# A graph kernel on Trainium2: in the first edge layer GpSimd also waits for the sums of two groups earlier before it gathers a group

## The reference

```python
edge_index = jnp.stack([src, dst])
h = jnp.maximum(_layernorm(x), 0.0)
# layer 0, a graph convolution
xw = h @ W
dinv = rsqrt(segment_sum(ones, dst) + ...)        # 1/sqrt(degree)
x = x + relu(segment_sum(xw[src] * (dinv[src] * dinv[dst])[:, None], dst) + b)
h = jnp.maximum(_layernorm(x), 0.0)
# layer 1, attention over the edges, 8 heads of 16
q, k, v = h[src] @ Wq.T + bq, h[dst] @ Wk.T + bk, h[dst] @ Wv.T + bv
e = exp(clip(einsum('ehd,ehd->eh', q, k) / sqrt(16), -10, 10))
out = segment_sum(e / (segment_sum(e, src)[src] + 1e-8) * v, src)
x = x + layernorm(out + h) * gamma + beta
```

## Time and profile before

| | us |
|---|---|
| timed runs, median of 3 | 2273.32 |
| timed runs, lowest and highest | 2272.0, 2273.41 |
| recorded execution, its span (the page gives no other time for it) | 2940.6 |

### The profile page before, as it was taken

How to read it: one execution, slowest core, us unless ns; L and a number is a source line. 1 busy time by engine, 2 the same in 40 slices (tenths; PEclk the granted TensorE clock), 3 DMA queues, 4 the chain that set the end, 5 groups by cost and what they waited for, 6 DMA issues and landing times. The chain is left out here.

```text
span 2940.6 us, 44304 instructions
## 1 busy us (share of the span) xinstructions
PE 1840.2 (63%) x10257; PEld 1461.4 (50%) x10258; DVE 1874.7 (64%) x5089; ACT 1279.6 (44%) x3362; POOL 1551.0 (53%) x1594
## 2 busy tenths in 40 slices
PE   5323346767576676677776767676666676666662
PEld 4323334544344444344454656566556665656662
DVE  9858775655455755455775666666666666666666
ACT  8524345755465565556653323333223332322333
POOL 0256655665556565565434555545455555555544
PEclk7756667877778787878887888888888888888886
DMA  3211111111111111111116444445444544444453
GB/s 105 62 41 42 43 39 39 45 42 38 38 38 45 38 41 41 39 44 39 33 68 185 126 125 127 127 122 131 119 121 124 132 123 122 125 123 123 126 122 55
DMA packets 234145, 244.06 MB, mean 83 GB/s; under 512 B 32925, under 2 KB 195229, under 8 KB 233989
## 3 DMA queue, kind: packets, MB, share of 16 engines
q0 software_dynamic: 61136, 147.00, 18.5%
q1 hardware_dynamic: 142357, 81.55, 10.8%
q10 hardware_dynamic: 30624, 15.21, 2.2%
HBM read 225.01 MB, written 18.62 MB: 83 GB/s over the span
## 5 line engine op out<-in xcount | busy, mean ns | idle before, releaser
L303 POOL DMA_INDIRECT rows<-y_tab,idx x832 | 795.6, 956 | 589.8 <-issue 307.9
L1340 POOL DMA_INDIRECT x<-kv_tab,kv_idx x672 | 682.7, 1016 | 623.0 <-DVE msg L1392 403.9
L1563 PE MATMUL ps_kv<-kv_s,hot_low 128*128 x1362 | 406.0, 443 | 168.9 <-DVE hot_low L1364 90.0
L780 ACT ACTIVATE sort_v<-sort_t,staged,minus 128x128 f16<-128x128 f16 x914 | 360.7, 480 | 309.1 <-remote 243.1
L872 PE MATMUL ps_sort<-sort_hi,sort_v 128*128 128x496 f16 x1662 | 417.6, 403 | 117.3 <-issue 112.4
L619 DVE TENSOR_SCALAR sort_v<-iota_h,staged 128x128 f16<-128x128 f16 x748 | 243.2, 325 | 339.2 <-remote 269.0
L1550 PE MATMUL ps_m<-msg,x 128*128 128x136 f32 x1792 | 295.4, 315 | 243.4 <-DVE msg L1392 182.7
L830 PE MATMUL ps_sum<-rows,hot 128*128 128x128 f32 x1664 | 282.0, 323 | 250.3 <-issue 120.1
L1374 DVE TENSOR_TENSOR by_tile<-ps_q,x 128x512 f32<-128x512 f32 x224 | 154.5, 690 | 404.9 <-remote 257.4
L830 PEld LDWEIGHTS ps_sum<-rows,hot 128*128 128x128 f32 x1664 | 260.4, 235 | 271.8 <-issue 139.4
L1550 PEld LDWEIGHTS ps_m<-msg,x 128*128 128x128 f32 x1792 | 263.3, 219 | 263.1 <-issue 245.7
(11 more groups left out here) (290 smaller groups left out, 2072.2 us busy)
## 6 DMA issues: line engine op xcount, KB each, us to landing
weights<-tile_tab SPq DMA_DIRECT2D x114, 256.0 KB
x<-tile_tab SPq DMA_DIRECT2D x113, 256.0 KB
weights<-tile_tab ACTq DMA_DIRECT2D x58, 256.0 KB
rows<-y_tab,idx POOLq DMA_INDIRECT x832
x<-kv_tab,kv_idx POOLq DMA_INDIRECT x672
kv_tab<-kv_s SPq DMA_DIRECT2D x12, 512.0 KB
x<-x_in SPq DMA_DIRECT2D x1, 3328.0 KB, 13.3
out<-x SPq DMA_DIRECT2D x12, 256.0 KB
```

The lines of the kernel that those rows point to most:

```text
L303: pool.indirect_dma_start(out=rows[:, k * SPAN + n, :], out_offset=None, in_=y_tab, in_offset=bass.IndirectOffsetOnAxis(ap=idx[:, k, n:n + ...
L780: last = nc.scalar.activation(to[:, k % 2, m, :], sort_t[:, k % 2, m, :], ACT.Relu, bias=staged[:, v, c:c + 1], scale=minus[:, v, c:c + 1])
L1340: pool.indirect_dma_start(out=rows[:, u, k, :], out_offset=None, in_=kv_tab, in_offset=bass.IndirectOffsetOnAxis(ap=idx[:, u, k:k + 1], ax ...
L1563: last = nc.tensor.matmul(ps_kv[:, k % 2, :], hot_low[:, w, k * P:(k + 1) * P], kv_s[:, ds(low + w, 1), :], start=w == 0, stop=w == WINDOW ...
```

## The change

Ahead of the 8 gathers of group g GpSimd waits for one semaphore more: the sums of group g - 2. For k = 2 and 3 these are sums of the same body, for k = 0 and 1 of the body before. The waits that were there stay. In the second edge layer the three loads behind SP's loop wait through a register that is first made positive, with an instruction that does nothing behind it (`wait_positive`); those inside the loop wait as before.

```diff
@@ -297,6 +297,7 @@
                     for k in range(GROUPS):
 
                         pool.wait_ge(sum_done[k], i + 1)
+                        pool.wait_ge(sum_done[(k - 2) % GROUPS], i + (1 if k < 2 else 2))
                         pool.wait_ge(idx_set[k], i + 1)
                         pool.nop(nofuse=True)
                         for n in range(SPAN):
@@ -1314,9 +1315,9 @@
-                def load_src(i, u):
-
-                    sp.wait_ge(off_made, i * QUADS + u + 1)
+                def load_src(i, u, after=sp.wait_ge):
+
+                    after(off_made, i * QUADS + u + 1)
@@ -1326,7 +1327,7 @@
                 for u in range(QUADS - 1):
-                    load_src(passes, u)
+                    load_src(passes, u, lambda semaphore, value: wait_positive(sp, semaphore, value))
```

## The result

| | before | with the change |
|---|---|---|
| median | 2272.7 us (4 runs, 2272.0 to 2273.41) | 2295.55 us (4 runs, 2294.57 to 2298.16) |
| recorded execution: its own time | not given | 2294.57 us |
| recorded execution: its span | 2940.6 us | 2292.9 us |

The change costs 22.9 us: a ratio of 1.010, with a 95% interval from 1.009 to 1.011. Forecast were 20.0 us more, 2293 us.

What follows compares the result with a forecast made beforehand. The prediction took GpSimd's gathers to pace both edge layers. A head start lost once, +20.0 us, with all other terms at 0, took 2273.3 us to 2293.3 us; the range was 2262 to 2350 us.

Steps and rivals of the forecast that it cites:

- The head start: Hole in TensorE's sums ahead of the sort stage: GpSimd enters the stage two groups later, +20.0 us (0 to 20.0).
- The steady loop: Sort stage once running: sums of g - 2 end in time, spare 4 to 6 us, 3.5 at body's end; 0 us.
- the later release: GpSimd's gather waits: one met a few us ahead costs 0 to 1.95 us, up to 160 us; taken as 0.
- the wait itself: One more wait per group in GpSimd's queue: at most 31 us, taken as 0, covered by queued gathers.
- It repeats in each body: Rival, slower: at body's end group 2 starts 2.3 us late, 21 bodies, 48 us, in all 2341 us; chance 0.25.
- Hidden: Rival, no change: gathers faster unrecorded or another engine sets the pace, so GpSimd waits anyway, 2273 us; chance 0.20.
- Faster through shorter bursts: Rival, sort stage: breaking up long gather runs frees TensorE's slow stretches, 2263 us; chance 0.15.
- The floor of 2262.9 us: Whole kernel: sum of terms with every gather at 1.25 us, 10.4 us below the measured median.
- The reading of the 667.3 us: Recorded span 2940.6 us against timed median 2273.3 us: the difference is not there when nothing is recorded.
- Waits for sums grow to hundreds: Sign in the changed profile: GpSimd's waits for sums grow from 61.0 us to hundreds.
- The sign at group 4: Ranking stage, changed profile: group 4's gathers start after group 2's sums, about 185 us, not 160.34.
- The sign at group 22: Start of the sort stage, changed profile: group 22's gathers start after group 20's sums.

Runs made afterwards that it cites:

- e6: GpSimd's new wait in body 5 alone (groups 20 to 23), plus the SP part, against the kernel before: 2284.78 us, ratio 1.0054.
- e7: GpSimd's new wait in bodies 10 to 25 alone, plus the SP part, against the kernel before: 2276.34 us, ratio 1.0007.
- e8: Only SP's three changed waits, no new GpSimd wait, against the kernel before, session at 2273 us: 2274.94 us, ratio 1.0008.
- distance three: Wait in all bodies for sums of group g - 3, plus the SP part, against the kernel before: 2865.82 us, ratio 0.9859; again 2861.24 us, 0.9883.
- e1: Only SP's three changed waits, no new GpSimd wait, against the kernel before, session at 2900 us: 2907.83 us, ratio 1.0011.

## Why the prediction was right, and which of its steps were not

**The mechanism is the one forecast.** GpSimd paces the first edge layer, so gathers that stood in the hole ahead of the sort stage and now stand behind it are lost once. Group 22 starts 0.8 us after the sums of group 20 end (356.4 and 357.21 us). The wait there is the longest, e6 with the wait in that one body has 10 to 15 of the 20 us, and e7 with the wait in 16 later bodies has 1.4 in the median and 4.6 at its last gather.

**The head start, forecast +20.0, measured 15.4 us at group 24.** Group 24 starts at 377.25 instead of 361.87. The term counted two whole groups, from a trace in which GpSimd too stood idle in the hole, 4.24 and 12.13 us. At 2273 us it does not: it works its way into the hole without a pause, and when the sums of group 20 end at 356.3 it has gathered group 22 and half of group 23, which ends at 361.6. That is twelve gathers, 15.0 us at 1.25, and not sixteen. This is the term of the sum that was mis-sized.

**A place that the prediction did not see** brings the rest: the hole between the two halves of the sort, +3.8 us, a further instance of the same mechanism. It had also not seen two waits in the ranking stage, 1.5 and 1.7 us, but these add nothing to the end. Without them, in e6, GpSimd reaches the hole earlier and waits there for longer, and group 24 starts at 377.28 us, with them at 377.25: the sums of group 20 decide. Along the way about 3 us come and go: group 22 starts 16.9 us later and group 65 (790.2 instead of 776.3 us) 13.9 us later, since single gathers take up to 1.70 us beside the column work and these fall differently. So 20.0 was near the total because a term too large and an omission nearly cancelled. That part is luck. Of the 22.9 us of the first measurement the trace accounts for the 18.4 us by which the spans differ, from e8, whose recorded execution was itself 3.5 us above the median before; against e8's median, in its own session, the full change costs 17.7 us.

**The steady loop, the later release, the wait itself: 0, measured 0.** In the sort stage with the change, the sums of group g - 2 end 1.4 to 6.8 us before the gathers of group g start, except for groups 22 and 66 at the two holes, and each time the gap ahead of the gathers is the usual 0.30 us. The forecast had 4 to 6 us and 3.5 us at a body's end; the least is 2 us smaller. The row with 1.95 us per release, up to 160 us in all, was read at 2900 us; at 2273 us nothing like it occurs. It repeats in each body (rival, 0.25): does not happen; e7 excludes it.

**Hidden (rival, 0.20): fell**, by the 22.9 and 19.5 us measured in two sessions. **Faster through shorter bursts (rival, 0.15): fell at 2273 us**, where there are no slow stretches to free. At 2900 us partial waits did gain 1.1 to 1.4%, but the larger gain (distance three) came with 240 us of gaps against 265, the smaller one with 148: that fewer such gaps are what gains is not shown. The full change was not run there.

**The floor of 2262.9 us was right in total and wrong in its terms.** Set beside e8:

| term | forecast us | e8 us |
|---|---|---|
| outside the gather stages | 302.4 | 294.9 |
| from 120 to the end of group 20's sums | 298.3 | 236.3 |
| the gathers that remain then | 800 | 813.2 |
| from the last gather to the end of the layer's sums | 22.2 | 5.0 |
| second edge layer | 840 | 925.1 |

(813.2 is 1169.5 - 356.3, in which GpSimd has 645 gathers to do and not 640.) The ranking stage was taken from the trace at 2900 us and is 62 us shorter. The second layer is 85 us longer than its gathers at 1.25 us, because its gathers of 1 KB take 1.07 us each. GpSimd's line for it in e8 (count, busy time, mean ns, idle time and what ended it; 19.4 us of that stand ahead of the first gather):

```profile
L1340 POOL DMA_INDIRECT x<-kv_tab,kv_idx x672 | 715.3, 1064 | 230.2 <-issue 173.1 <-DVE msg L1392 37.7 <-ACT kv_idx L1472 19.4
```

Gathers of 715.3 us and 671 usual gaps, 201.3 us, are 916.6 of the 926.1 us from its first gather to the end of its last. So at 2273 us this layer runs at GpSimd's pace too, within 9.5 us, as the prediction had it; only the price of a gather was taken from the other layer. That both layers are at this pace is shown by how little GpSimd pauses in e8; the total did not prove it, as the prediction itself had noted.

**The reading of the 667.3 us was wrong.** The prediction put them down to recording. The recorded executions at 2273 us have spans of 2292.9 and 2274.5 us and times of their own of 2294.57 and 2276.18 us, within 1.3 us of the medians: no cost of recording is seen here. This agrees with the Trainium skill (NOTIFIC — the notification-queue block, Constraints, capacities, measured rates), by which an implicit record costs the engine no cycles. So the 667.3 us are the difference between two sessions; e1, the same kernel but for SP's waits, has a span of 2906.7 us in a session of 2897.5. The prediction had set that page aside because of the total, and with it the thought that the slow stretches are real; they are, but not in the runs that were timed, so the forecast held for a reason that it did not know.

**"Waits for sums grow to hundreds": wrong.** They are 19.6 us, seven times. If GpSimd paces the stage it can't wait for hundreds of microseconds; the sentence took the recorded 12.9 us per group for granted, against the prediction's own theory. **The sign at group 4 failed as well:** it was to start at about 185 us instead of 160.34, and it starts at 160.62, as in e8 (160.55). At 2273 us the sums of group 2 end at 157.7 us, not at 184.8, so the new wait finds them done. The sign at group 22 held, and no wait for indices is left, but e8 has only 0.9 us of those. What TensorE waits for rows also grew, in the sums of `ps_more` and `ps_sum`; with the change, then in e8:

```profile
PE ps_more L831 <- DMA rows<-y_tab,idx: 125.3, 32, 8.3
PE ps_sum L831 <- DMA rows<-y_tab,idx: 113.1, 27, 26.8
```

```profile
PE ps_more L830 <- DMA rows<-y_tab,idx: 104.9, 27, 8.3
PE ps_sum L830 <- DMA rows<-y_tab,idx: 99.6, 24, 26.8
```

Together 33.9 us more, while waits for the one-hot matrices shrank: TensorE now waits for the gathers at places where it used to wait for VectorE.

**What stays open.** What sets a session at 2900 us, and what holds TensorE between matmuls there; of the gaps above 0.8 us in e1's sort stage 188 of 244 us lie where GpSimd has issued more than 8 gathers on end, though such runs make up only 295 us of the 1043; no experiment separates the gathers' issue from their transfers. Why distance three gains there is open as well. Whether distance three is free at 2273 us was not measured, nor does a run at that speed have the wait in body 16 alone. No kernel here beats the kernel before at 2273 us.

## What to carry to other kernels

Where an engine works through its queue without a pause, a pause that a new wait puts into it is not won back, and it is looked for at the holes in the consumer's work, not in the steady loop: there a depth of two groups was as good as four. A small pause ahead of a larger one added nothing here, since the release that ends the larger one came no later for it. What a hole costs is the work that the engine used to get done in it. Before a difference between a recorded span and a timed median is put down to the recorder, compare the span with that execution's own time; without that number, terms from the trace are terms of another speed. A total that comes out right is weak evidence for its terms: here one of them was 62 us too large and another 85 us too small.

## What the hardware showed that was not expected

The same kernel on the same chip took 2273.2 us in one session and 2897.5 us in another. In the slower one, TensorE's granted clock in the sort stage is 0.80 instead of 0.89, but its busy time grows only by 710.4 - 648.1 = 62 us of the 225 us by which the stage is longer; the gaps between matmuls without a releaser come to 265 us, more than the other 163 us, so in part they stand where TensorE waited for rows and matrices at the other speed. In the second edge layer a clock of 0.84 for 0.99 goes with 149 us more busy time and 352 us more time. A change that loses 0.9% at one speed has relatives (the same wait from body 10 on, or at distance three) that gain over 1% at the other and, as far as it was measured, nothing at the first.
